# An adaLN block on one core: the second layer norm of tiles 4 to 7 moved from the first half into the second half's first pass

## The chip, the core and the metric

The kernel runs on one core of one Trainium2 chip. A core has TensorE (PE, matmuls into PSUM), VectorE (DVE), ScalarE (ACT), GpSimd (POOL) and SyncE (SP, which only issues DMAs here). Each engine takes its own instructions in order; they meet at semaphores. The metric is the device time of one execution in microseconds.

## The reference

```python
mod = (_silu(c) @ wmod).reshape(B, 6, 1, -1)             # sa, ca, ga, sb, cb, gb for each of 4 batches
h = _layernorm(x) * (1 + ca) + sa
q = h @ Wq.T;  sigma_q = elu(q) + 1                       # 16 heads of 32
a = einsum('bhsd,nhde->nbhse', sigma_q, memories) / clip(einsum('bhsd,nhd->nbhs', sigma_q, memory_norms), 1e-6)
attn = einsum('nbhse,hn->bhse', a, softmax(bank_weights)) @ Wo.T
x = x + ga * attn
h = _layernorm(x) * (1 + cb) + sb                         # the second norm
h = silu(h @ w_gate) * (h @ w_up)
h = h where it is one of the two largest of its group of 4, else 0
x = x + gb * (h @ w_down)
```

x is 4 x 1024 tokens of 512 floats, the hidden size of the FFN 2048. Everything is float32; the kernel splits each factor into a high and a low part and adds three products (high x high, low x high, high x low).

## The kernel before, in words

The 4096 tokens are 8 tiles of 512, a tile is four subtiles of 128. The program has two halves, and each engine's order is written out by hand.

**First half (attention, 0 to about 320 us).** `tile(t)` runs once per tile on every engine, some 35.2 us each. TensorE makes the products with the norms, then for each subtile the four memory banks (`banks_of`), the transpose of their sum (`comb_transpose`) and the product with Wo (`wo_product`), and q of the next tile. VectorE scales the banks (L1065, `banks_r`), splits off the low part of the transposed sum (L1030, `combT_lo`), and adds the result into x (L1019 and L1024). POOL sums the banks (L469, L474). The second norm of tile t-1 runs inside tile t: `late_stats` (L889, bn_stats of a subtile) and `ln_aggregate` (L893) on VectorE, `ln_sqrt` (L566), `normalize` (L560) and `split_bits` (L610, which puts the two 16-bit halves of each float into separate columns) on ScalarE. SP then stores the bits to DRAM, from where a transposing DMA brings them back in the second half. Tile 7's norm is finished beside the first matmuls of the second half.

**Second half (FFN, from about 304 us).** There are 16 passes `tile_b(t2)` of 65.3 us: tiles 0 to 7 with hidden columns 0 to 1023 (passes 0 to 7), then again with 1024 to 2047. A pass has two chunks (cc = 0, 1). For each, TensorE makes four pairs of gate and up products (`gate_or_up`, j = 0 to 3, two pairs of banks used in turn) and, one chunk behind, the down product (`down`). ScalarE takes silu of a gate (L789), VectorE multiplies with up (L1157), ScalarE takes the absolute value (L795), and when all four are there VectorE finds the two largest of each four (`sparsify`, L1179 to L1198). ScalarE (L774) and POOL (L506) split the result for `down`. The inputs of the next tile, h2, are joined from the transposed bits on ScalarE (`join_h2`, L747 and L751) during the pass. Their high part (`h2_high`, L757) can only be written when the pass's last up product has been read, and POOL makes the low part (`h2_low`, L457, `h_lo` in the trace) while TensorE is in the last down product. Pass 0 is written out apart; it also splits the weights of the first two chunks (`split_w`, L739, as `w_raw` arrives).

SP issues its DMAs in order, each behind its waits: a load that stands behind `store_bits(t)` waits until ScalarE has copied the bits of tile t.

## Time and profile before

| | us |
|---|---|
| median of 3 runs | 1367.31 |
| lowest and highest | 1366.39, 1367.68 |
| the profiled execution, its own time | 1366.45 |
| its span (first to last instruction) | 1364.6 |
| TensorE busy / VectorE / ScalarE / POOL | 1341.1 / 847.0 / 637.8 / 564.3 |

The span is what the trace covers; the execution's own time is 1.85 us more. Matmuls are pipelined, so each is drawn longer (0.39 us) than the step to the next (0.226 us): a gap in TensorE's stream is read from the starts, not from the busy time. The granted TensorE clock is 0.999 of full speed over the span.

### The profile page before, as it was taken

To read this page: it belongs to the slowest core of one execution; us is meant where nothing else is said; L and a number is where in the kernel's file an instruction comes from. 1 tells how busy PE (TensorE), PEld (TensorE's weight loads), DVE (VectorE), ACT (ScalarE), POOL (GpSimd) and SP (SyncE) were. 2 spreads that over 40 slices of the span, in tenths; PEclk is the share of its full clock that TensorE was granted. 3 is DMA by queue.
4 is the path that set the end of the run, shared out by engine and by line. 5 is a ranking of instruction groups with operands and counts; after the bars stand their busy time and mean duration, and the time that the engine had idled before them with its cause. 6 is when DMAs were issued, how large, how long until landed. Compare 5 with 4: busy or idle time off the path is not lost.

```text
span 1364.6 us, 18637 instructions
## 1 busy us (share of the span) xinstructions
PE 1341.1 (98%) x6726; PEld 1098.6 (81%) x6726; DVE 847.0 (62%) x1220; ACT 637.8 (47%) x933; POOL 564.3 (41%) x428
## 2 busy tenths in 40 slices
PE   7899999999999999999999999999999999999998
PEld 6777777777788888888888888888888888888887
DVE  6878888886746364645555575765555646363646
ACT  6677777787543343434343444433333333343321
POOL 2877777770733141414141456543232323231412
PEclk9999999999999999999999999999999999999999
DMA  6422222136202020202030322322020202020102
GB/s 256 155 93 93 92 92 81 73 93 222 79 16 85 15 85 15 85 15 85 27 88 31 100 89 89 110 68 85 15 85 15 85 15 85 15 85 15 69 0 100
DMA packets 91422, 102.43 MB, mean 75 GB/s; under 512 B 68960, under 2 KB 69504, under 8 KB 84864
## 3 DMA queue, kind: packets, MB, share of 16 engines
q1 hardware_dynamic: 91392, 102.05, 23.0%
q8 instruction: 16, 0.26, 0.1%
q14 instruction: 14, 0.11, 0.0%
HBM read 51.69 MB, written 33.57 MB: 62 GB/s over the span
## 4 chain that ended last, share of the span: by engine, by line
PE 86%; DVE 8%; ACT 2%; issue 2%; POOL 1%; DMA 1%; SPq 0%; DVEq 0%; ACTq 0%; POOLq 0%
PE bank L1252 27%; PE bank L1254 27%; PE bank L1253 27%; DVE banks_r L1065 3%; PE bank L1327 2%; PE bank L1339 1%; DVE inv_norm L1053 1%; POOL h_lo L457 1%; PE bank L1280 1%; DMA wmod_sb<-in_wmod_dram 1%; PE bank L1303 1%; DVE ln_raw L889 0%; DVE h_abs L1198 0%; DVE combT_lo L1030 0%; DVE xn L985 0%
## 5 line engine op out<-in xcount | busy, mean ns | idle before, releaser
L1157 DVE TENSOR_TENSOR h_act<-bank,silu_g 128x512 f32<-128x512 f32 x128 | 88.3, 690 | 411.8 <-PE bank L1254 385.7
L506 POOL TENSOR_TENSOR hs_lo<-h_abs,hs_hi 128x512 fp32r<-128x512 f32 x124 | 170.0, 1401 | 381.4 <-ACT hs_hi L774 381.4
L774 ACT ACTIVATE hs_hi<-h_abs 128x512 fp32r<-128x512 f32 x124 | 72.7, 627 | 323.7 <-DVE h_abs L1198 200.8
L457 POOL TENSOR_TENSOR h_lo<-h_raw,h_hi 128x512 fp32r<-128x512 f32 x62 | 122.2, 1999 | 233.2 <-ACT h_hi L757 233.2
L1252 PE MATMUL bank<-h_hi,gate_w_hi 128*128 128x512 f32 x512 | 199.7, 390 | 1.8 <-POOL h_lo L457 1.5
L1252 PE MATMUL bank<-h_hi,up_w_hi 128*128 128x512 f32 x512 | 199.5, 390 | 0.7 <-DVE h_act L1157 0.7
L1253 PE MATMUL bank<-h_lo,gate_w_hi 128*128 128x512 f32 x512 | 199.2, 389 | 0.0
L1253 PE MATMUL bank<-h_lo,up_w_hi 128*128 128x512 f32 x512 | 199.2, 389 | 0.0
L1254 PE MATMUL bank<-h_hi,up_w_lo 128*128 128x512 f32 x512 | 199.2, 389 | 0.0
L1254 PE MATMUL bank<-h_hi,gate_w_lo 128*128 128x512 f32 x512 | 199.2, 389 | 0.0
L1252 PE MATMUL bank<-down_w_hi,hs_hi 128*128 128x512 f32 x496 | 192.9, 389 | 0.0
L1253 PE MATMUL bank<-down_w_lo,hs_hi 128*128 128x512 f32 x496 | 192.9, 389 | 0.0
L1254 PE MATMUL bank<-down_w_hi,hs_lo 128*128 128x512 f32 x496 | 192.9, 389 | 0.0
L789 ACT ACTIVATE silu_g<-bank 128x512 f32<-128x512 f32 x128 | 75.9, 595 | 216.7 <-PE bank L1254 216.6
L1252 PEld LDWEIGHTS bank<-h_hi,gate_w_hi 128*128 128x128 f32 x512 | 96.2, 188 | 23.5 <-POOL h_lo L457 2.3
L1252 PEld LDWEIGHTS bank<-h_hi,up_w_hi 128*128 128x128 f32 x512 | 96.1, 188 | 21.6 <-DVE h_act L1157 1.1
L1254 PEld LDWEIGHTS bank<-h_hi,up_w_lo 128*128 128x128 f32 x512 | 96.2, 188 | 20.0
L1254 PEld LDWEIGHTS bank<-h_hi,gate_w_lo 128*128 128x128 f32 x512 | 96.1, 188 | 20.0
L1253 PEld LDWEIGHTS bank<-h_lo,up_w_hi 128*128 128x128 f32 x512 | 96.1, 188 | 19.9
L1253 PEld LDWEIGHTS bank<-h_lo,gate_w_hi 128*128 128x128 f32 x512 | 96.1, 188 | 19.6
L795 ACT ACTIVATE h_abs<-h_act 128x512 f32<-128x512 f32 x128 | 80.0, 625 | 68.0 <-DVE h_act L1157 68.0
L1254 PEld LDWEIGHTS bank<-down_w_hi,hs_lo 128*128 128x128 f32 x496 | 93.1, 188 | 19.3
(149 smaller groups left out, 2472.7 us busy)
## 6 DMA issues: line engine op xcount, KB each, us to landing
x_ring<-in_x_dram SPq DMA_DIRECT2D x8, 1024.0 KB, 4.9
x_scratch<-x_ring SPq DMA_DIRECT2D x8, 1024.0 KB, 3.9
xn_bits_scratch<-set_up_stage SPq DMA_DIRECT2D x8, 1024.0 KB, 4.5
over_x<-x_scratch SPq DMA_DIRECT2D x8, 1024.0 KB, 4.9
acc_scratch<-over_x SPq DMA_DIRECT2D x8, 1024.0 KB, 3.9
over_x<-acc_scratch SPq DMA_DIRECT2D x8, 1024.0 KB, 4.9
out_dram<-over_x SPq DMA_DIRECT2D x7, 1024.0 KB, 3.9
w_raw<-in_w_gate_dram SPq DMA_DIRECT2D x4, 1024.0 KB, 6.0
```

The lines of the kernel that those rows point to most:

```text
L457: nc.gpsimd.tensor_tensor(h2_lo[:, k], h2_raw[:, k], h2_hi[:, k].bitcast(F32), ALU.subtract).then_inc(h2_lo_done, 1)
L506: nc.gpsimd.tensor_tensor(hs_lo[:, j], h_abs[:, j], hs_hi[:, j].bitcast(F32), ALU.subtract).then_inc(hs_lo_done, 1)
L774: nc.scalar.activation(hs_hi[:, j], h_abs[:, j], ACT.Copy).then_inc(hs_hi_done, 1)
L789: nc.scalar.activation(silu_g[:, j % 2], bank[2 * (j % 2)][:], ACT.Silu).then_inc(silu_done, 1)
L795: nc.scalar.activation(h_abs[:, j], h_act[:, cc, j], ACT.Abs).then_inc(abs_done, 1)
L1053: nc.vector.reciprocal(inv, inv).then_inc(recip_done, 1)
L1065: nc.vector.tensor_tensor(scaled[:, g // 2, :, g % 2], bank[g][:].rearrange("p (i a e) -> p i a e", i=2, e=DH), r[:, g // 2, :, g % 2].uns ...
L1157: nc.vector.tensor_tensor(h_act[:, cc, j], bank[2 * (j % 2) + 1][:], silu_g[:, j % 2], ALU.mult).then_inc(h_done, 1)
L1252: nc.tensor.matmul(out_, stat[0], mov[0], start=start, stop=False)
L1253: nc.tensor.matmul(out_, stat[0], mov[1], start=False, stop=False)
L1254: return nc.tensor.matmul(out_, stat[1], mov[0], start=False, stop=stop)
L1327: ins = nc.tensor.matmul(bank[2 * two + pair][:, cols], stat[rows, g, toks], mov[rows, g], start=first, stop=last)
```

## The change

`EARLY = 4` divides the tiles. Tiles 0 to 3 keep their second norm in the first half (in tiles 1 to 4 of the loop, `norm2`). Tiles 4 to 7 get none there: no statistics, root, normalization or bit copies, and SP's loads and stores no longer wait for them. Instead pass t2 of the second half (t2 = 1 to 4) prepares tile t2 + 3, one subtile after the other in one buffer `late_x1`, in these steps: ScalarE issues a load of 256 KB of x1 from DRAM (`late_load`); VectorE takes statistics (`late_norm`); ScalarE takes the root (`late_root`); VectorE the reciprocal and shift (`late_scalars`); ScalarE normalizes, copies the bits, and issues their store and the next load (`late_split`). The loops of ScalarE and VectorE are divided in two for it, and `load_bits` waits for the four stores of a tile. `eps_col` moves to memory that lives through both halves.

```diff
@@ -173,6 +174,14 @@
         up_w[1] = in_halves("up_w1", [P, K, J, P])
         down_w[0] = in_halves("down_w0", [P, J, D])
         down_w[1] = in_halves("down_w1", [P, J, D])
+        late_x1 = sbb("late_x1", [P, D])
+        late_raw = sbb("late_raw", [P, 6])
+        late_mv = sbb("late_mv", [P, 2])
+        late_sd = sbb("late_sd", [P, 1])
+        late_rstd = sbb("late_rstd", [P, 1])
+        late_shift = sbb("late_shift", [P, 1])
+        late_pad = sbb("late_pad", [P, 1])
+        late_bits = over_x1_rest[:, 3].bitcast(U16)
 
 
         small_in, norm_in, wq_in, wo_in = map(sem, ("small_in", "norm_in", "wq_in", "wo_in"))
...
@@ -299,8 +308,10 @@
                 sp.wait_ge(bits_done, 4 * t + 4)
                 sp.dma_start(bits_dram[t].rearrange("(s p) c -> p s c", p=P), xn2_bits).then_inc(bits_out, 16)
 
-            def load_bits(t2, half, tile=None):
+            def load_bits(t2, half, tile=None, late=False):
                 tile = t2 if tile is None else tile
+                if late:
+                    sp.wait_ge(bits_out, 64 * tile + 16 * (4 - 3 * EARLY))
                 sp.dma_start(bitsT.rearrange("p k h n -> p (k h) n"), bits_dram[tile][:, half * D:(half + 1) * D],
                              transpose=True).then_inc(bits_in, 16)
 
...
@@ -316,24 +327,24 @@
                                  transpose=True).then_inc(bits_in, 16)
                 store_x1(t - 1)
                 if t + 2 < NT:
-                    sp.wait_ge(xn2_done, 4 * t)
+                    if t <= EARLY:
+                        sp.wait_ge(xn2_done, 4 * t)
                     sp.wait_ge(x1_out, 16 * t)
                     sp.dma_start(x_ring[:, place(t + 2)], x_t[t + 2]).then_inc(x_in[place(t + 2)], 16)
                 if t == 1:
                     sp.wait_ge(w_lo_dve, 1)
                     load_w((0, 1))
                 if t == NT - 1:
-                    sp.wait_ge(xn2_done, 4 * t)
                     sp.wait_ge(x1_out, 16 * t)
                     load_w((1, 1))
                     sp.wait_ge(w_lo_dve, 2)
                     load_w((1, 0))
-                store_bits(t - 1)
+                if t <= EARLY:
+                    store_bits(t - 1)
             store_x1(NT - 1)
-            sp.wait_ge(xn2_done, 4 * NT)
             sp.wait_ge(x1_out, 16 * NT)
+            sp.wait_ge(bits_out, 16 * EARLY)
             load_bits(1, 0)
-            store_bits(NT - 1)
 
 
             sp.wait_ge(w_lo_dve, 3)
...
@@ -362,7 +373,7 @@
                 store_y(acc_t, t - 1, t - 1)
                 load_y(x1_t, t)
                 sp.wait_ge(bits_joined, 4 * t + 8)
-                load_bits(t + 2, 0)
+                load_bits(t + 2, 0, late=True)
 
             t = NT - 2
             sp.wait_ge(bits_joined, 4 * t + 6)
...
@@ -699,16 +710,13 @@
                             transposed()
                         else:
                             h1_split(t + 1, before_last=transposed, part=None if first else 1)
-                        if not first and not last:
+                        if norm2:
                             ln_sqrt(t - 1, 1)
                             normalize(t - 1, 1, xn2, xn2_done)
                     if s == 3:
-                        if not first and not last:
+                        if norm2:
                             split_bits(t - 1, (0, 1))
                         transposed()
-                        if last:
-                            normalize(t - 1, 1, xn2, xn2_done)
-                            split_bits(t - 1, (0, 1))
 
                     if last and s == 0:
                         for k in (0, 1):
...
@@ -760,7 +764,9 @@
 
             act.wait_ge(wa_lo, 1)
             act.wait_ge(mods_ready, 2)
-            with act.Fori(1, NT - 1) as t:
+            with act.Fori(1, EARLY + 1) as t:
+                tile(t, norm2=True)
+            with act.Fori(EARLY + 1, NT - 1) as t:
                 tile(t)
             tile(NT - 1, last=True)
             combT_high(4 * NT - 1, 1)
...
@@ -805,36 +811,76 @@
                     if j in between:
                         between[j]()
 
-            def tile_b(t2, tile=None, last=False):
+            def late_load(tile, s):
+                act.wait_ge(bits_done, 4 * tile + s)
+                nc.scalar.dma_start(late_x1[:], x1_t[tile, :, s]).then_inc(late_in, 16)
+
+            def late_root(tile, s):
+                act.wait_ge(ag2_done, 4 * tile + s + 1)
+                nc.scalar.activation(late_sd[:], late_mv[:, 1:2], ACT.Sqrt, bias=eps_col[:]).then_inc(sd_done[1], 1)
+
+            def late_split(tile, s):
+                index = 4 * tile + s - 3 * EARLY
+                act.wait_ge(shift_done[1], index + 1)
+                nc.scalar.activation(late_x1[:], late_x1[:], ACT.Identity, bias=late_shift[:],
+                                     scale=late_rstd[:]).then_inc(xn2_done, 1)
+                act.wait_ge(xn2_done, 4 * tile + s + 1)
+                act.wait_ge(bits_out, 16 * index)
+                words = late_x1[:].bitcast(U16).rearrange("p (k d h) -> p k h d", k=K, h=2)
+                nc.scalar.activation(late_bits.rearrange("p (k h d) -> p k h d", k=K, h=2), words,
+                                     ACT.Copy).then_inc(bits_done, 1)
+                act.wait_ge(bits_done, 4 * tile + s + 1)
+                nc.scalar.dma_start(bits_dram[tile][s * P:(s + 1) * P], late_bits).then_inc(bits_out, 16)
+                if s < S - 1:
+                    late_load(tile, s + 1)
+
+            def tile_b(t2, tile=None, last=False, late=False):
                 def join(k):
                     return lambda: join_h2(t2 + 1, tile, k)
 
+                def between(cc):
+                    if last:
+                        return {}
+                    if not late:
+                        return {0: join(2 * cc), 1: join(2 * cc + 1)}
+
+                    def join_and_root():
+                        join_h2(t2 + 1, tile, 2 * cc)
+                        late_root(t2 + 3, 2 * cc)
+
+                    def join_and_split():
+                        join_h2(t2 + 1, tile, 2 * cc + 1)
+                        late_split(t2 + 3, 2 * cc)
+
+                    return {0: join_and_root, 1: join_and_split, 3: lambda: late_root(t2 + 3, 2 * cc + 1)}
+
+                if late:
+                    late_load(t2 + 3, 0)
                 hs_high(2 * t2 - 1)
-                item(2 * t2, 0, {} if last else {0: join(0), 1: join(1)})
+                item(2 * t2, 0, between(0))
+                if late:
+                    late_split(t2 + 3, 1)
                 hs_high(2 * t2)
-                item(2 * t2 + 1, 1, {} if last else {0: join(2), 1: join(3)})
+                item(2 * t2 + 1, 1, between(1))
                 if not last:
                     act.wait_ge(up_done, 8 * t2 + 8)
                     h2_high(t2 + 1)
-
-            last_tile = NT - 1
+                if late:
+                    late_split(t2 + 3, 3)
+
             silu(0, 0, first=True)
-            ln_sqrt(last_tile, 1)
             silu(0, 1, first=True)
-            normalize(last_tile, 1, xn2, xn2_done)
             split_w(SPLITS[2])
             absolute(0, 0, 0, first=True)
-            split_bits(last_tile, (0, 1))
             silu(0, 2)
             absolute(0, 0, 1, first=True)
-            split_bits(last_tile, (2, 3))
             act.wait_ge(x1_done, 4 * NT)
             split_w(SPLITS[3])
             silu(0, 3)
             absolute(0, 0, 2, first=True)
             absolute(0, 0, 3, first=True)
             silu(1, 0)
-            act.wait_ge(bits_out, 16 * NT)
+            act.wait_ge(bits_out, 16 * EARLY)
             split_w(SPLITS[4])
             silu(1, 1)
             join_h2(1, 1, 0)
...
@@ -1118,7 +1169,7 @@
                     combT_low(u, 0)
                     attn_rest(t - 1, 3, u - 1, stats=False)
                 scale_banks(u + 2, 0, first)
-                if not first:
+                if norm2:
                     late_stats(t - 1, 3, u - 1)
                     dve.wait_ge(bn2_done, 4 * t)
                     ln_aggregate(t - 1, 1, ag2_done)
...
@@ -1126,19 +1177,19 @@
                 if first:
                     dve.wait_ge(ga_in, 16 * B)
                 attn_rest(t, 0, u, stats=False)
-                if not first and not last:
+                if norm2:
                     ln_scalars(t - 1, 1)
 
                 scale_banks(u + 3, 1, first)
                 if last:
-                    ln_scalars(t - 1, 1)
                     dve.wait_ge(h2_lo_done, 2)
                     for k in (2, 3):
                         dve.wait_ge(h2_hi_done, k + 1)
                         nc.vector.tensor_tensor(h2_lo[:, k], h2_raw[:, k], h2_hi[:, k].bitcast(F32),
                                                 ALU.subtract).then_inc(h2_lo_done, 1)
-                late_stats(t, 0, u)
-                attn_rest(t, 1, u + 1, between=lambda: combT_low(u + 2, 0))
+                if t < EARLY:
+                    late_stats(t, 0, u)
+                attn_rest(t, 1, u + 1, between=lambda: combT_low(u + 2, 0), stats=t < EARLY)
                 if first:
                     dve.wait_ge(mods_mm, 2)
                     nc.vector.tensor_copy(mods[:, 2], mm2[:, 0])
...
@@ -1208,28 +1259,48 @@
                     dve.wait_ge(y_scaled, 4 * t2 + s + 1)
                     nc.vector.tensor_tensor(y[:, s], bank[4 + s][:], y[:, s], ALU.add).then_inc(y_done, 1)
 
-            def tile_b(t2, last=False):
+            def late_norm(tile, s):
+                dve.wait_ge(late_in, 16 * (4 * (tile - EARLY) + s + 1))
+                nc.vector.bn_stats(late_raw[:], late_x1[:]).then_inc(bn2_done, 1)
+                dve.wait_ge(bn2_done, 4 * tile + s + 1)
+                nc.vector.memset(late_pad[:], 0.0)
+                nc.vector.bn_aggr(late_mv[:], late_raw[:]).then_inc(ag2_done, 1)
+
+            def late_scalars(tile, s):
+                index = 4 * tile + s - 3 * EARLY
+                dve.wait_ge(sd_done[1], index + 1)
+                nc.vector.reciprocal(late_rstd[:], late_sd[:]).then_inc(rstd_done[1], 1)
+                dve.wait_ge(rstd_done[1], index + 1)
+                nc.vector.scalar_tensor_tensor(out=late_shift[:], in0=late_mv[:, 0:1], scalar=-1.0, in1=late_rstd[:],
+                                               op0=ALU.mult, op1=ALU.mult).then_inc(shift_done[1], 1)
+
+            def tile_b(t2, last=False, late=False):
                 for cc in range(SLOTS):
                     n = 2 * t2 + cc
                     for j in range(J):
                         hidden_act(n, cc, j)
+                        if late and j == 0:
+                            late_norm(t2 + 3, 2 * cc)
                         if cc == 1 and j == 1:
                             add_ffn(t2 - 1)
+                        if late and j == 1:
+                            late_scalars(t2 + 3, 2 * cc)
+                        if late and j == 3:
+                            late_norm(t2 + 3, 2 * cc + 1)
                     if last and cc == 1:
                         for half in range(2):
                             sparsify(n, cc, toks=LAST_HALVES[half], half=half)
+                    elif late:
+                        sparsify(n, cc, between=lambda: late_scalars(t2 + 3, 2 * cc + 1))
                     else:
                         sparsify(n, cc)
 
 
             split_w_low(SPLITS[1])
-            attn_rest(NT - 1, 2, 4 * NT - 2)
+            attn_rest(NT - 1, 2, 4 * NT - 2, stats=False)
             combT_low(4 * NT - 1, 1)
             hidden_act(0, 0, 0)
-            attn_rest(NT - 1, 3, 4 * NT - 1)
-            dve.wait_ge(bn2_done, 4 * NT)
-            ln_aggregate(NT - 1, 1, ag2_done)
-            ln_scalars(NT - 1, 1)
+            attn_rest(NT - 1, 3, 4 * NT - 1, stats=False)
             hidden_act(0, 0, 1)
             split_w_low(SPLITS[2])
             hidden_act(0, 0, 2)
...
@@ -1239,7 +1310,9 @@
             for j in range(1, J):
                 hidden_act(1, 1, j)
             sparsify(1, 1)
-            with dve.Fori(1, NT2 - 1) as t2:
+            with dve.Fori(EARLY - 3, NT - 3) as t2:
+                tile_b(t2, late=True)
+            with dve.Fori(NT - 3, NT2 - 1) as t2:
                 tile_b(t2)
             tile_b(NT2 - 1, last=True)
             add_ffn(NT2 - 1)
```

**VectorE, last tile of the first half,** from the scaling of the last banks to the low part of the first up weights (`up_w_lo`). Before:

```order
L1065 TENSOR_TENSOR banks_r<-bank,inv_norm 128x2x256 x4
L898 RECIPROCAL ln_rstd<-ln_sd 128x4
L900 SCALAR_TENSOR_TENSOR ln_shift<-ln_mv,ln_rstd 128x4
L1138 TENSOR_TENSOR h_lo<-h_raw,h_hi 128x512 x2
L889 BN_STATS ln_raw<-x_ring 128x6
L1019 TENSOR_TENSOR bank<-bank,ga_all 128x512
L1030 TENSOR_TENSOR combT_lo<-bank,combT_hi 128x512
L1024 TENSOR_TENSOR x_ring<-bank,x_ring 128x512
L889 BN_STATS ln_raw<-x_ring 128x6
L1037 TENSOR_TENSOR up_w_lo<-w_raw,up_w_hi 128x2048
```

Now (line numbers of the changed kernel):

```order
L1114 TENSOR_TENSOR banks_r<-bank,inv_norm 128x2x256 x4
L1188 TENSOR_TENSOR h_lo<-h_raw,h_hi 128x512 x2
L1068 TENSOR_TENSOR bank<-bank,ga_all 128x512
L1079 TENSOR_TENSOR combT_lo<-bank,combT_hi 128x512
L1073 TENSOR_TENSOR x_ring<-bank,x_ring 128x512
L1086 TENSOR_TENSOR up_w_lo<-w_raw,up_w_hi 128x2048
```

The scalars of tile 6 and two statistics of tile 7 are gone; what is left keeps its order.

**ScalarE, end of a pass of the second half,** from the last absolute values to the jump back (h_hi is h2's high part for the next tile). Before:

```order
L795 ACTIVATE h_abs<-h_act 128x512 x2
L817 ISA
L757 ACTIVATE h_hi<-h_raw 128x512 x4
L847 REGISTER_ALU
L847 COMPARE_AND_BRANCH
```

Now, in passes 1 to 4:

```order
L801 ACTIVATE h_abs<-h_act 128x512 x2
L819 REGISTER_ALU
L820 ACT_TABLE_LOAD
L820 ACTIVATE late_sd<-late_mv,eps_col 128x1
L866 ISA
L761 ACTIVATE h_hi<-h_raw 128x512 x4
L824 REGISTER_ALU
L825 ACTIVATE late_x<-late_x,late_shift,late_rstd 128x512
L828 REGISTER_ALU
L830 ACTIVATE over_x<-late_x 128x1024
L833 ISA
L833 DMA xn_bits_scratch<-over_x 128x1024
```

A table load and a root stand in front of h_hi, and a normalization, a bit copy and a store behind it.

**ScalarE, start of the next pass,** from the loop's entry to the first silu. Before:

```order
L774 ACTIVATE hs_hi<-h_abs 128x512
L786 ISA
L788 REGISTER_ALU
L789 ACTIVATE silu_g<-bank 128x512
```

Now:

```order
L816 DMA late_x<-x_scratch 128x512
L777 ISA
L779 REGISTER_ALU
L780 ACT_TABLE_LOAD
L780 ACTIVATE hs_hi<-h_abs 128x512
...
L792 ISA
L794 REGISTER_ALU
L795 ACT_TABLE_LOAD
L795 ACTIVATE silu_g<-bank 128x512
```

The load of the first subtile and two table loads are new here (the first also in passes 5 and 6). One of four hs_hi is shown.

## Rows read from the trace of the kernel before

**Rows 1.** The page, busy times (1) and the chain that ended last (4), by engine.

```profile
PE 1341.1 (98%) x6726; PEld 1098.6 (81%) x6726; DVE 847.0 (62%) x1220; ACT 637.8 (47%) x933; POOL 564.3 (41%) x428
...
PE 86%; DVE 8%; ACT 2%; issue 2%; POOL 1%; DMA 1%; SPq 0%; DVEq 0%; ACTq 0%; POOLq 0%
```

**Rows 2.** Stretches: start:end us, length, busy us (instructions), TensorE clock, DMA share, GB/s.

```profile
400.00:500.00 100.00, 100.00 (x443) 82.84 (x442) 55.17 (x67) 37.08 (x56) 31.86 (x20) 1.00 0.20 63
...
420.00:424.00 4.00, 4.00 (x19) 3.30 (x19) 0.00 (x0) 1.12 (x2) 0.00 (x0) 1.00 0.63 262
```

**Rows 3.** TensorE in order of time: start, us, engine, line, operation [idle <- releaser].

```profile
224.47 0.28 PE L1327 MATMUL bank<-mem_lo,sigma_hi 64*128 64x256 f32 x2
224.85 0.50 PE L1252 MATMUL bank<-wo_hi,combT_hi 128*128 128x512 f32 x1
...
336.40 0.50 PE L1252 MATMUL bank<-h_hi,up_w_hi 128*128 128x512 f32 x1
```

**Rows 4.** The same view, the four large gaps.

```profile
308.17 0.51 PE L1252 MATMUL bank<-wo_hi,combT_hi 128*128 128x512 f32 x1 [0.82 <-DVE combT_lo L1030]
...
353.70 0.50 PE L1252 MATMUL bank<-h_hi,up_w_hi 128*128 128x512 f32 x1 [0.68 <-DVE h_act L1157]
...
368.56 0.39 PE L1254 MATMUL bank<-h_hi,gate_w_lo 128*128 128x512 f32 x1
369.69 0.50 PE L1252 MATMUL bank<-h_hi,gate_w_hi 128*128 128x512 f32 x1 [0.74 <-POOL h_lo L457]
...
371.38 0.50 PE L1252 MATMUL bank<-h_hi,gate_w_hi 128*128 128x512 f32 x1 [0.72 <-POOL h_lo L457]
```

**Rows 5.** VectorE, ScalarE and POOL in order of time, where those gaps come from.

```profile
306.25 0.68 DVE L889 BATCH_NORM_STATS2 ln_raw<-x_ring 128x6 f32<-128x512 f32 x1
...
340.66 1.92 ACT L739 ACTIVATE down_w_hi<-w_raw 128x2048 fp32r<-128x2048 f32 x1 [2.56 <-DMA w_raw<-in_w_down_dram]
...
363.38 7.94 POOL L457 TENSOR_TENSOR h_lo<-h_raw,h_hi 128x512 fp32r<-128x512 f32 x4 [1.69 <-ACT h_hi L757]
```

**Rows 6.** Groups by shape: count | busy us, mean ns | idle before.

```profile
L610 ACT ACTIVATE set_up_stage<-xn 128x1024 uint16<-128x1024 uint16 x32 | 31.7, 1042 | 0.0
...
L566 ACT ACT_TABLE_LOAD x10 | 12.8, 1283 | 0.2
...
L560 ACT ACTIVATE xn<-x_ring,ln_shift,ln_rstd 128x512 f32<-128x512 f32 x16 | 11.7, 803 | 4.6 <-DVE ln_shift L900 4.6
...
L893 DVE BATCH_NORM_AGGREGATE ln_mv<-ln_raw 128x2 f32<-128x6 f32 x64 | 6.0, 156 | 0.3
...
L566 ACT ACTIVATE ln_sd<-ln_mv,eps_col 128x4 f32<-128x4 f32 x16 | 4.7, 292 | 10.1 <-DVE ln_mv L893 10.0
```

**Rows 7.** SP's queue at 419.51 (issue time), and DMA issues: KB each, us to landing.

```profile
419.51 0.37 SPq L349 DMA_DIRECT2D acc_scratch<-over_x  x1
...
over_x<-gates_scratch SPq DMA_DIRECT2D x16, 256.0 KB, 5.8
...
out_dram<-over_x SPq DMA_DIRECT2D x4, 256.0 KB, 2.5
```

**Rows 8.** The end of pass 1 and start of pass 2, in order of time, three engines.

```profile
425.44 2.18 ACT L757 ACTIVATE h_hi<-h_raw 128x512 fp32r<-128x512 f32 x4
...
426.13 7.98 POOL L457 TENSOR_TENSOR h_lo<-h_raw,h_hi 128x512 fp32r<-128x512 f32 x4 [18.04 <-ACT h_hi L757]
...
436.83 0.39 PE L1252 MATMUL bank<-h_hi,gate_w_hi 128*128 128x512 f32 x1
...
441.45 0.58 ACT L789 ACTIVATE silu_g<-bank 128x512 f32<-128x512 f32 x1
...
445.67 0.39 PE L1252 MATMUL bank<-h_hi,gate_w_hi 128*128 128x512 f32 x1
```

**Rows 9.** ScalarE in order of time, around one table load.

```profile
203.16 1.28 ACT L620 ACT_TABLE_LOAD   x1
204.46 0.63 ACT L620 ACTIVATE exp_q<-exp_q 128x512 f32<-128x512 f32 x1
```

More of the change, by code:

```diff
@@ L48 @@
 SA, CA, GA, SB, CB, GB = range(6)
+EARLY = 4
 def adaln_kernel(nc, x, wqT, woT, bank_w, mem_hd, norm_hd, w_gate, w_up, w_down, cT, wmod, out):
@@ L78, in adaln_kernel @@
         mods = ctx.enter_context(nc.sbuf_tensor("mods", [P, 4, K, B], F32))
+        eps_col = ctx.enter_context(nc.sbuf_tensor("eps_col", [P, 1], F32))
         gate_w, up_w, down_w = [None] * SLOTS, [None] * SLOTS, [None] * SLOTS
@@ L137, in adaln_kernel @@
             ln_mv = sba("ln_mv", [P, 2, S, 2])
-            eps_col = sba("eps_col", [P, 1])
             ln_sd = sba("ln_sd", [P, 2, S])
@@ L203, in adaln_kernel @@
         wo_done, attn_scaled_done, x1_done = map(sem, ("wo_done", "attn_scaled_done", "x1_done"))
-        xn2_done, bits_done = map(sem, ("xn2_done", "bits_done"))
+        xn2_done, bits_done, late_in = map(sem, ("xn2_done", "bits_done", "late_in"))
         w_in = [sem(f"w_in{i}") for i in range(3 * CHUNKS)]
@@ L675, in copy_row, with tile @@
                 nc.scalar.activation(mod_rows[:, i], bank[5 + 2 * i][:, 0:P], ACT.Copy).then_inc(rows_done, 1)
-            def tile(t, first=False, last=False):
+            def tile(t, first=False, last=False, norm2=False):
                 for s in range(S):
@@ L721, in tile @@
                         h2_high(0, (s + 1,))
-                    if last and s == 2:
-                        ln_sqrt(t - 1, 1)
                     if first and s == 3:
@@ L727, in h2_rest @@
                 def h2_rest():
-                    if not first:
+                    if norm2:
                         split_bits(t - 1, (2, 3))
-                if last:
-                    h2_rest()
-                else:
+                if not last:
                     sigma_all(t + 1, between=h2_rest, before_high=lambda: combT_high(4 * t + 3, 1))
@@ L846, in _ @@
             h2_high(1)
-            with act.Fori(1, NT - 1) as t2:
+            act.wait_ge(x1_out, 16 * NT)
+            with act.Fori(EARLY - 3, NT - 3) as t2:
+                tile_b(t2, t2 + 1, late=True)
+            with act.Fori(NT - 3, NT - 1) as t2:
                 tile_b(t2, t2 + 1)
@@ L1074, in tile @@
                 u = 4 * t
+                norm2 = 1 <= t <= EARLY
                 def stats(*subtiles):
@@ L1107, in tile @@
                     scale_banks(u, 0, between=next_scalars)
-                    late_stats(t - 1, 2, u - 2)
+                    if norm2:
+                        late_stats(t - 1, 2, u - 2)
                 invert_norms(t, 1)
@@ L1120, in tile @@
                 scale_banks(u + 2, 0, first)
-                if not first:
+                if norm2:
                     late_stats(t - 1, 3, u - 1)
@@ L1128, in tile @@
                 attn_rest(t, 0, u, stats=False)
-                if not first and not last:
+                if norm2:
                     ln_scalars(t - 1, 1)
```

## The prediction

> **What bounds the kernel now.** I read the page's busy times and chain first, then the stretches, then TensorE's instructions in order of time, then the engines it waits for. TensorE is busy for 98% of the span and makes up 86% of the chain that ended last [rows 1]. From 400 us on it has no idle time, with a matmul every 0.226 us: 100.00 of 100 us for 443 of them [rows 2]; the waits that are listed for it lie before 372 us and in the last tile. So only two things can move the time: gaps in TensorE's stream before about 372 us, which the change may close, and new gaps in the second half, which it may open. The other engines have room: DVE 847 us, ScalarE (ACT) 638 us, GpSimd (POOL) 564 us of 1364.6 [rows 1].
>
> The gaps are read as steps between the starts of neighbouring matmuls, since the modelled ends hide short ones. Seven small ones lie where VectorE has a step of the second norm, or a weight split behind one, ahead of what TensorE waits for. The first of them is the step from 224.47 to 224.85, 0.38 us where 0.23 is usual, and the last is at 336.40 [rows 3]. With about 0.15 us each at 224.85, 260.05 and 294.96, 0.05 at 300.26, 0.3 at 306.38 and 311.69, and 0.2 at 336.40 they hold 1.3 us. The large ones are at 308.17 (0.82 us idle for combT_lo), 353.70 (0.68 for h_act), and 369.69 and 371.38 (0.74 and 0.72 for h_lo) [rows 4]. The last one's neighbour shows the true cost: from 368.56 to 369.69 is 1.13 us, 0.90 more than a usual step, and the first step behind a gap is another 0.1 longer. So these four cost 1.0, 0.95, 1.0 and 1.0 us.
>
> **What is removed.** In the first half tiles 4 to 7 lose 16 bn_stats of 0.68 us, 16 aggregates of 0.16, 16 normalizing activations of 0.80, 16 bit copies of 1.04 and four roots of 0.29 [rows 5, 6]. That is 13 us of VectorE and 31 us of ScalarE. Nearly all of it lies beside matmuls; only what stands in front of something late counts, and there are four places.
>
> 1. Tiles 5, 6 and 7: one bn_stats (0.68 us) stood between two groups of banks_r. Without it combT_lo comes in time, but the wait for POOL's combined stays, since POOL starts it from an earlier banks_r. I take the small gaps at 0.15, 0.15, 0.15 and 0.05 us.
> 2. Around 305 us VectorE runs scalars, h_lo, a bn_stats at 306.25, a product, and only then combT_lo [rows 5]. Without the statistics and the aggregate at 299 us, combT_lo ends near 306.8, not just before 308.17. TensorE is free near 306.8 too, so all of the 1.0 us at 308.17 goes, with 0.3 at 306.38 and 0.3 at 311.69, where up_w_lo was the last.
> 3. ScalarE spends 3.2 us from 322 us on normalizing tile 7 and 4.2 on its bit copies [rows 6], and SP issues its loads in order behind them: the first down weights are used at 340.66, after a wait of 2.56 us for their transfer [rows 5]. With both gone these weights are asked for near 324, so their split starts near 335 and ends near 337. The sparsification then starts 4 us earlier. VectorE still shares its time with POOL's weight split, ends near 348, and h_act is there before TensorE wants it at 351.0. The 0.95 us at 353.70 goes, and the 0.2 at 336.40.
> 4. The same chain brings POOL's four h_lo for tile 1 from 363.38 to about 359.0, while TensorE comes 2.7 us earlier. They take 7.94 us [rows 5], so the fourth ends at 367.0 and is wanted at 366.6. Of 2.0 us 0.4 stays and 1.6 goes.
>
> Sum of the gains: 1.3 + 1.0 + 0.95 + 1.6 = 4.85 us. From below this is 0 (something else is as late), from above 6 us: all 5.25 us of these gaps, and a little of those that POOL sets.
>
> **What is added.** Each of the four passes 1 to 4 of the second half now prepares a tile in four subtiles. ScalarE gets, per subtile, a root (0.29), a normalization (0.80), a bit copy (1.04), two DMA issues, and table loads of 1.28 us [rows 6, 7]. The order shows nine loads a pass: four for roots, four for silu behind them, one at the loop's start. One issue takes SP 0.37 us [rows 7]; ScalarE's own is not in the trace of before, and I take the same, with 0 below and 1.5 above. Per pass that is 9 x 1.28 + 4 x 2.13 + 8 x 0.37 = 23 us, on an engine that works some 24 of a pass's 65.3 us. VectorE gets 1.2 us per subtile. So neither becomes the bound; only the order matters. TensorE writes four banks in turn and needs a silu or product about 8 us after it has finished the matmuls for it, which covers 5 us of insertions in the middle of a pass. The tight place is the end of the pass, in two respects.
>
> **h_lo of the next tile.** Before, ScalarE goes from the last h_abs to h_hi at 425.44, POOL's four h_lo run from 426.13 to 434.11, and TensorE wants the fourth at 436.83 [rows 8]: 2.7 us of room. Now a table load and a root stand in front, 1.28 + 0.29 + 0.1 = 1.7 us, and h_lo ends near 435.9. Room left is 0.9 us. The root also waits for VectorE's statistics, which wait for the fourth subtile's transfer. ScalarE issues it near 422.6, behind the store of the third. The nearest rows are 2.5 us for 256 KB alone and 5.8 us for 256 KB issued behind 1 MB [rows 7]. I take 3.0, nearer to the first, since y's 1 MB load is issued only at 424: it lands near 425.6, the aggregate is there at 426.6, and the table load hides it.
>
> **The first silu of the next pass.** It starts at 441.45 now and is wanted at 445.67 [rows 8], where the third gate group starts: with its 0.6 us, 3.6 us of room. In front of it come 1.1 us of VectorE (statistics ahead of sparsification), 0.4 of scalars inside sparsification, 0.3 because ScalarE's last bit copy, two issues and the loop's table load run until about 440.5, and 1.28 for silu's own table. That is 3.1 us, and 0.5 is left.
>
> Both margins are smaller than what I can be wrong by, so I count 0.2 us lost per pass, 0.8 in all, with 0 and 9 as ends. Other waits are covered: the bits of a tile are written one pass before SP asks for them, and passes 5 and 6 get two table loads each, with 3.6 us of room.
>
> **A rule weighed.** At 203.16 a table load takes 1.28 us and the exponential starts at 204.46, 0.02 us behind it [rows 9]. So here a switch costs 1.3 us. The Trainium skill (ScalarE: Activation LUTs, What ACT_TABLE_LOAD costs) puts a drain of 1380 ns on top of the load, 2.66 us for each switch. By that rule the added loads would cost 96 us instead of 46, and both margins would be gone; the trace disagrees with it.
>
> **Sum.** The profiled execution took 1366.45 us around a span of 1364.6. Less 4.85, plus 0.8, its own time becomes 1362.4. The median of the runs is 0.86 us above it, so I forecast 1363.3 us, 0.3% faster. Runs of this kernel differ by 1.3 us, so I call anything within 0.2% (2.7 us) no change.
>
> **Rivals.**
> - *The ends of the passes give it back* (0.22). If ScalarE's issues or the waits among the four handovers per subtile cost 1 us more than I took, TensorE waits about 1 us at each of four ends: 1363.3 + 4 = 1367. For it: margins of 0.5 to 0.9 us, and a chain in which each subtile waits for ScalarE, VectorE and a DMA in turn. Against it: VectorE and ScalarE catch up in the middle of a pass, so it doesn't add up.
> - *The fourth subtile lands late, and it is slower* (0.13). If its transfer shares the engines with y's store and load, as the gate row's did, it takes 5.8 us. It lands at 428.4, the root ends at 429.7, the fourth h_lo at 438.5: 1.6 us of waiting, and 0.6 more at the first silu. That is 2.2 us a pass, 8.8 in all, so 1367.3 - 4.85 + 8.8 = 1371. It decides from a landing of 4.2 us on. For it: the DMA engines are 63% busy from 420 to 424 us in the trace [rows 2]. Against it: the queued 1 MB is not in front but behind.
> - *A table switch holds ScalarE about twice as long as its load* (0.03). With 1.3 us more for each, h_lo is late by 0.4 and silu, behind three switches, by 3.4 beyond its room: 3.5 us a pass, 14 in all, 1376. The pair at 203.16 speaks against it. This is the time that the rule of the Trainium skill (ScalarE: Activation LUTs, What ACT_TABLE_LOAD costs) would make.
> - *The gaps before 372 us stay* (0.07). If loads from HBM and not ScalarE set the down weights' arrival, the 0.95 and 1.6 us stay, and 2.3 - 0.8 = 1.5 us are gained: 1365.8.
> - *My forecast*, 1361 to 1364.6, has 0.55.
>
> Its own range is 1361.0 to 1364.6. The range over the cases is 1360.6 to 1370.5. Chances: faster 0.59 (the forecast, and a part of the first and fourth rivals), same 0.25, slower 0.16.
>
> **What would show it.** In the new profile no idle time in front of combT_lo's product near 308, none near 352 and 370 or at most 0.5 us; ScalarE's down_w_hi near 335; nine table loads a pass of 1.28 us; POOL's fourth h_lo ending within 1 us of the gate group that reads it; PE waits in four places at a distance of 65 us, short or absent. I am wrong if TensorE waits over 1 us at each of these, if a DMA issue on ScalarE takes over 1 us, or if the gaps before 372 us are still there.

## The result and the profile after

The changed kernel takes 1374.97 us (median of 5 runs, 1371.39 to 1375.59) against 1367.09 us (1366.39 to 1367.68) before: a ratio of 1.0050, with a 95% interval of 1.0039 to 1.0062. It is slower, where 1363.3 us and 0.3% faster were forecast. It lies outside the forecast's own range of 1361.0 to 1364.6 and outside the range over the cases, 1360.6 to 1370.5. The profiled execution took 1371.39 us around a span of 1369.6, the fastest of the five. The other four have no trace: in them up to 4.2 us more were lost, and where is not shown.

The page's busy times of the changed kernel and its chain that ended last, against [rows 1]:

```profile
PE 1344.3 (98%) x6726; PEld 1099.2 (80%) x6726; DVE 850.3 (62%) x1260; ACT 693.1 (51%) x982; POOL 561.3 (41%) x428
...
PE 66%; issue 18%; POOL 7%; DVE 6%; ACT 2%; DMA 1%; POOLq 0%; ACTq 0%; SPq 0%; DVEq 0%
```

ScalarE (ACT) has 55 us more of work, and TensorE's share of the chain fell from 86 to 66%. The stretches of [rows 2] show where:

```profile
400.00:500.00 100.00, 97.99 (x430) 80.19 (x429) 60.15 (x95) 65.57 (x86) 29.13 (x19) 1.00 0.33 94
...
420.00:424.00 4.00, 4.00 (x20) 3.30 (x19) 0.69 (x1) 3.03 (x4) 0.00 (x0) 1.00 0.78 197
```

TensorE made 443 matmuls in these 100 us before and makes 430 now, at the same full clock: 13 x 0.226 = 2.9 us are missing. From 700 us on it is back at 443. So the loss lies in passes 1 to 4, those that prepare a late tile. TensorE in order of time, at the first place of [rows 4] and around the start of pass 2 ([rows 8]):

```profile
306.07 0.50 PE L1325 MATMUL bank<-h_hi,gate_w_hi 128*128 128x512 f32 x1 [0.18 <-DVE h_lo L1188]
...
307.27 0.50 PE L1325 MATMUL bank<-wo_hi,combT_hi 128*128 128x512 f32 x1 [0.24 <-DVE combT_lo L1079]
...
433.31 0.50 PE L1325 MATMUL bank<-h_hi,gate_w_hi 128*128 128x512 f32 x1 [0.55 <-POOL h_lo L468]
...
434.99 0.50 PE L1325 MATMUL bank<-h_hi,gate_w_hi 128*128 128x512 f32 x1 [0.71 <-POOL h_lo L468]
...
444.87 0.50 PE L1325 MATMUL bank<-h_hi,gate_w_hi 128*128 128x512 f32 x1 [0.75 <-ACT silu_g L795]
```

The gap at 353.70 is gone, of the two near 370 one step is left that is 0.30 us longer than usual (at 367.37), and that at 308 is down to 0.24. In their place pass 1 ends with two waits for h_lo, at 433.31 and 434.99, and passes 2, 3 and 4 with one each (0.72 at 502.40, 0.69 at 569.73, 0.70 at 637.17). The third gate group of the next pass waits for silu at 444.87, 512.28 and 579.60 (0.73 to 0.75 us each). By the starts each of these costs 0.70 to 0.91 us. From the list of TensorE's waits by releaser (us in total, times, longest) of the changed kernel:

```profile
...
PE bank L1325 <- POOL h_lo L468: 3.4, 5, 0.7
PE bank L1412 <- POOL combined L485: 3.1, 8, 1.1
PE bank L1325 <- ACT silu_g L795: 2.7, 5, 0.8
```

What holds them, at the end of pass 1, in order of time (ACTq and SPq rows are DMA issues; L355 is the load of y, L816 that of a subtile):

```profile
419.95 0.37 ACTq L816 DMA_DIRECT2D late_x<-x_scratch  x1
420.00 0.35 SPq L355 DMA_DIRECT2D over_x<-x_scratch  x1
420.49 0.60 ACT L795 ACTIVATE silu_g<-bank 128x512 f32<-128x512 f32 x1 [1.23 <-issue]
...
425.62 0.69 DVE L1264 BATCH_NORM_STATS2 late_raw<-late_x 128x6 f32<-128x512 f32 x1 [3.81 <-DMA late_x<-x_scratch]
...
426.46 1.19 DVE L1230 TENSOR_TENSOR pair_hi<-h_abs 128x1024 f32<-128x1024 f32 x1
426.57 0.29 ACT L820 ACTIVATE late_sd<-late_mv,eps_col 128x1 f32<-128x1 f32 x1 [2.79 <-DVE late_mv L1267]
426.78 2.18 ACT L761 ACTIVATE h_hi<-h_raw 128x512 fp32r<-128x512 f32 x4
427.47 7.46 POOL L468 TENSOR_TENSOR h_lo<-h_raw,h_hi 128x512 fp32r<-128x512 f32 x4 [19.01 <-ACT h_hi L761]
427.57 2.32 DVE L1231 TENSOR_TENSOR pair_lo<-h_abs 128x1024 f32<-128x1024 f32 x1
...
435.79 0.82 ACT L825 ACTIVATE late_x<-late_x,late_shift,late_rstd 128x512 f32<-128x512 f32 x1 [6.83 <-DVE late_shift L1274]
...
438.87 0.35 ACTq L816 DMA_DIRECT2D late_x<-x_scratch  x1
439.41 1.28 ACT L780 ACT_TABLE_LOAD   x1 [1.64 <-issue]
440.71 2.20 ACT L780 ACTIVATE hs_hi<-h_abs 128x512 fp32r<-128x512 f32 x4
...
442.92 1.28 ACT L795 ACT_TABLE_LOAD   x1
444.22 1.09 ACT L795 ACTIVATE silu_g<-bank 128x512 f32<-128x512 f32 x2
```

The load of the fourth subtile and y's load leave within 0.05 us of each other. In the next three passes they are 0.24, 0.23 and 0.20 us apart, and the landings are 5.05 to 5.11 us: a pass that is late moves both, and they meet again. VectorE stands idle for the subtile until 425.62, 5.67 us behind the issue. Two things queue behind it: on ScalarE the root and then h2_high, on VectorE the whole sparsification. From bn_stats to the next pass's first silu, 18.60 us, every step waits for the one before: sparsification beside GpSimd's h_lo, normalise, bit copy, two issues, a table load, hs_hi, a second table load.

### The profile page after: what moved, and what is told of

The parts are those of the page before. It is cut to its first block, busy times and chain, and to the rows that moved or that the text cites. A ratio compares the mean times of both kernels' runs of the same rounds, so it can differ in the third digit from the quotient of the medians.

```text
span 1369.6 us, 18878 instructions
## 1 busy us (share of the span) xinstructions
PE 1344.3 (98%) x6726; PEld 1099.2 (80%) x6726; DVE 850.3 (62%) x1260; ACT 693.1 (51%) x982; POOL 561.3 (41%) x428
## 4 chain that ended last, share of the span: by engine, by line
PE 66%; issue 18%; POOL 7%; DVE 6%; ACT 2%; DMA 1%; POOLq 0%; ACTq 0%; SPq 0%; DVEq 0%
PE bank L1325 21%; PE bank L1327 21%; PE bank L1326 20%; POOL hs_lo L517 2%; POOL h_lo L468 2%; DVE banks_r L1114 2%; PE bank L1400 2%; PE bank L1412 1%; POOL sigma_lo L453 1%; POOL banks_r L480 1%; PE bank L1353 1%; DMA wmod_sb<-in_wmod_dram 1%; DVE h_abs L1249 0%; POOL combined L485 0%; DVE inv_norm L1102 0%
## 5 line engine op out<-in xcount | busy, mean ns | idle before, releaser
L1326 PEld LDWEIGHTS bank<-down_w_lo,hs_hi 128*128 128x128 f32 x496 | 93.1, 188 | 19.4
```

The costliest lines, as they stand in the source:

```text
L1326: nc.tensor.matmul(out_, stat[0], mov[1], start=False, stop=False)
```

## The experiments

All are compared with the kernel before on the same chip; the changed kernel was not run again beside them. The kernel before had medians of 1366.97 us (first four), 1367.16 (next three) and 1367.17 (last). "Landing" below is the time from the fourth subtile's issue on ScalarE to its bn_stats in pass 1, "chain" from there to the next first silu, "period" the step between passes in the trace. A "..." in an edit marks lines left out.

**first_half_only**: the late loops take the ordinary passes.

```diff
...
+                sp.dma_start(bits_dram[t + EARLY].rearrange("(s p) c -> p s c", p=P), xn2_bits).then_inc(late_in, 16)
...
-            with act.Fori(EARLY - 3, NT - 3) as t2:
-                tile_b(t2, t2 + 1, late=True)
-            with act.Fori(NT - 3, NT - 1) as t2:
+            with act.Fori(EARLY - 3, NT - 1) as t2:
...
```

> Leaves out the late steps of passes 1 to 4 (their loads, norms and bits stores); tiles 4 to 7 get no second norm of their own, the bits of tiles 0 to 3 are stored twice in their place, so that the second half has words to load. Theory: the first half gained what was forecast (4.85 us) and all of the loss is in passes 1 to 4, so without the late steps the time is 1362.3 us (1361.5 to 1363.5). Rival: the first half gained nothing that lasts to the end, and the time is that of before, 1367 us. Second rival: the first half itself is slower, over 1368 us.

Measured: 1362.79 us, ratio 0.9971 (0.9959 to 0.9984), period 65.28 us as before. The first half brought 4.2 us (1366.97 - 1362.79; 3.8 by the spans) and keeps it, where 4.85 were forecast. So the whole loss is made by the late steps: 8.8 us between the spans of this kernel (1360.8) and of the changed one (1369.6), 12 us between the medians. Only the profiled execution has a trace, so the 3.4 us between these two numbers stay without a cause.

**one_load**: the four subtiles come by one transfer at the start of the pass.

```diff
-        late_x1 = sbb("late_x1", [P, D])
+        late_x1 = w_raw[:].rearrange("p (s d) -> p s d", d=D)
...
-                nc.scalar.dma_start(late_x1[:], x1_t[tile, :, s]).then_inc(late_in, 16)
+                nc.scalar.dma_start(late_x1, x1_t[tile]).then_inc(late_in, 16)
...
-                if s < S - 1:
-                    late_load(tile, s + 1)
```

> The changed kernel with the whole x1 of a late tile fetched by one transfer at the start of the pass, into the weight staging that is free then: no subtile waits for its transfer, and three DMA issues per pass leave ScalarE. Theory (the late landing of the fourth subtile and the chain behind it cost the time): VectorE's waits of 3.8 and 3.3 us for late_x1 go, h2_high and sparsify start some 3 us earlier, both kinds of TensorE waits (h_lo, silu_g) go, and the time falls from 1375 to 1363 to 1366 us. Rival (ScalarE's added work itself, 16 normalises, copies, roots and table loads, costs it): only the three issues of about 0.5 us per pass go, 4 x 1.5 = 6 us of ScalarE at most and most of it in its idle time, so 1371 us or more.

Measured: 1363.35 us, ratio 0.9973 (0.9962 to 0.9983). VectorE in order of time in this kernel:

```profile
420.57 0.69 DVE L1207 TENSOR_TENSOR h_act<-bank,silu_g 128x512 f32<-128x512 f32 x1 [3.90 <-PE bank L1326]
421.18 0.68 DVE L1263 BATCH_NORM_STATS2 late_raw<-w_raw 128x6 f32<-128x512 f32 x1
```

No wait stands ahead of the fourth bn_stats, 4.4 us earlier than in the changed kernel. TensorE's waits for POOL's h_lo are off its list and those for silu_g down to 0.5 us in all, of which 0.2 at the start of pass 1. All sixteen roots, normalisations, bit copies and stores are still there, so ScalarE's work as such costs at most 0.6 us (1363.35 against the 1362.79 without late steps).

**high_first**: h2_high ahead of the fourth root.

```diff
+                    def high_and_root():
+                        if cc == 1:
+                            act.wait_ge(up_done, 8 * t2 + 8)
+                            h2_high(t2 + 1)
+                        late_root(t2 + 3, 2 * cc + 1)
...
-                if not last:
+                if not last and not late:
                     act.wait_ge(up_done, 8 * t2 + 8)
                     h2_high(t2 + 1)
```

> The changed kernel with h2_high ahead of the fourth subtile's root instead of behind it. Theory (late landing): the landing stays at 5 to 5.7 us, but TensorE's waits for h_lo (3.4 us over four passes in the trace) go; those for silu_g (2.7 us) stay or grow by up to 1 us a pass, since the root now comes 8.8 us later and holds VectorE's scalars in sparsify. Time 1370 to 1373 us. Rival (ScalarE's work as such): no change, 1374 to 1376 us.

Measured: 1363.58 us, ratio 0.9975 (0.9965 to 0.9984): better than the 1370 to 1373 expected, although the landing grew to 6.76 us (the load leaves 0.05 us behind y's here). VectorE and GpSimd (POOL) in this kernel:

```profile
423.33 5.04 POOL L468 TENSOR_TENSOR h_lo<-h_raw,h_hi 128x512 fp32r<-128x512 f32 x4 [14.59 <-ACT h_hi L761]
...
426.97 0.69 DVE L1270 BATCH_NORM_STATS2 late_raw<-late_x 128x6 f32<-128x512 f32 x1 [4.91 <-DMA late_x<-x_scratch]
...
429.37 1.21 DVE L1237 TENSOR_TENSOR pair_lo<-h_abs 128x1024 f32<-128x1024 f32 x1
...
431.64 0.68 DVE L1240 TENSOR_TENSOR both_of<-pair_lo,pair_hi 128x512 bf16<-128x512 f32 x1
```

I had expected silu to stay late. What I missed is that h_lo now falls into VectorE's wait for the transfer and is nearly over when sparsification starts. From pair_hi to the first both_of takes 3.84 us here (427.80 to 431.64) and 5.58 in the changed kernel (426.46 to 432.04), and the four h_lo take 5.04 against 7.46 us. The two both_of themselves take 0.68 us each instead of 1.76 and 1.75. Together VectorE is 3.9 us shorter from pair_hi to the scalars behind both_of (427.80 to 432.84, against 426.46 to 435.40), and that is what the chain lost: it fell from 18.60 to 14.68 us.

**y_after**: y's store waits for the fourth bn_stats, and with it y's load and what SP issues behind that.

```diff
             def store_y(dst, tile, t2, after=0):
+                if not isinstance(after, int):
+                    sp.wait_ge(bn2_done, after)
                 sp.wait_ge(y_done, 4 * t2 + 4)
...
-                store_y(acc_t, t - 1, t - 1)
+                store_y(acc_t, t - 1, t - 1, after=4 * t + 16)
```

> The changed kernel with the store and load of y in passes 1 to 4 held back until VectorE has read the fourth subtile. Theory (the 1 MB transfer of y shares the DMA engines with the 256 KB one): the fourth landing falls from 5.0 to 5.7 us to 3.1 to 3.6 us, h_lo's waits go and silu_g's shrink, time 1367 to 1371 us. Rival (the landing is late whatever else moves): landing still over 5 us, 1374 to 1376 us. Second rival: y's load now collides with the next steps (weights, bits of the next pass) and the time grows.

Measured: 1366.29 us, ratio 0.9996 (0.9987 to 1.0005), just below the 1367 to 1371 expected. Landing 3.52 us, and no wait for h_lo is left in the late passes. The chain is 18.62 us, and silu is still late, which the theory's estimate had allowed for; TensorE in this kernel:

```profile
443.03 0.50 PE L1335 MATMUL bank<-h_hi,gate_w_hi 128*128 128x512 f32 x1 [0.56 <-ACT silu_g L805]
```

The period is 66.1 us. So y's transfers, or those that SP issues behind them, make the landing late, and even with a landing of 3.5 us the first silu has no room.

**both**: the edits of one_load and high_first together.

> The single transfer of one_load and the order of high_first together. Theory: each alone already took TensorE's waits in the late passes down to 0.5 us, so nothing is left to gain: 1363 to 1364 us, as each alone. Rival (the two remove different losses that add): 1360 to 1361.5 us, below the kernel without late steps less its noise.

Measured: 1363.42 us, ratio 0.9973 (0.9963 to 0.9983), the same as each alone. The losses that they remove do not add.

**no_tables**: the root is left out, the table loads go with it.

```diff
-                nc.scalar.activation(late_sd[:], late_mv[:, 1:2], ACT.Sqrt, bias=eps_col[:]).then_inc(sd_done[1], 1)
+                nc.scalar.activation(late_sd[:], late_mv[:, 1:2], ACT.Identity, bias=eps_col[:]).then_inc(sd_done[1], 1)
```

> The changed kernel with the square root of the late norms left out: ScalarE copies the variance with eps added, so VectorE takes the reciprocal of that, and no table is loaded in the late passes. Theory (the fourth landing and GpSimd's h_lo beside sparsify cost the time): the load ahead of the fourth root lies in the wait for the landing, so h_lo's waits stay (3.4 us); the two loads of 1.28 us ahead of hs_high and the first silu leave that chain, its waits (2.7 us) go: 1371 to 1373 us. Rival (the sixteen roots with up to 1.28 us twice are the main cost): 1364 to 1367 us.

Measured: 1363.58 us, ratio 0.9975 (0.9966 to 0.9984). The theory's number was wrong; the rival's, 1364 to 1367, is nearer, and the time lies just below it. Landing is 5.07 us, but the issue comes 0.87 us earlier (419.08), and the chain is 15.94 us, 2.66 shorter, two table loads of 1.28. That is not proof that table loads are the main cost, since high_first and load_first keep all of them and come out at the same time: it is the same chain, shortened at another place.

**load_first**: the next subtile's load is issued ahead of the store.

```diff
                 act.wait_ge(bits_done, 4 * tile + s + 1)
+                if s < S - 1:
+                    nc.scalar.dma_start(late_x1[:], x1_t[tile, :, s + 1]).then_inc(late_in, 16)
                 nc.scalar.dma_start(bits_dram[tile][s * P:(s + 1) * P], late_bits).then_inc(bits_out, 16)
-                if s < S - 1:
-                    late_load(tile, s + 1)
```

> The changed kernel with each subtile's load issued ahead of the bits store of the one before, not behind it: the load leaves 0.5 us earlier. Theory: loss follows the fourth landing (1.9 us earlier brought 8.7 us over four passes in y_after), so 0.5 us earlier bring 1.5 to 2.5 us: 1372 to 1373.5 us. Rival (what counts is only whether the transfer of y is beside it, or the load now slows the store): 1375 us, no change.

Measured: 1363.70 us, ratio 0.9976 (0.9966 to 0.9985), far more than the 0.5 us of the edit. The issues in this kernel, and VectorE's wait:

```profile
419.51 0.34 ACTq L834 DMA_DIRECT2D late_x<-x_scratch  x1
...
420.87 0.35 SPq L355 DMA_DIRECT2D over_x<-x_scratch  x1
...
423.36 0.69 DVE L1264 BATCH_NORM_STATS2 late_raw<-late_x 128x6 f32<-128x512 f32 x1 [1.18 <-DMA late_x<-x_scratch]
```

The subtile's load now leaves 1.36 us ahead of y's, and lands in 3.85 us instead of 5.67; the chain is as long as ever (18.65 us). In the other three passes the leads are 1.33 to 1.37 us and the landings 3.69 to 3.95, and the late passes have none of TensorE's waits for h_lo.

The lead is larger than the 0.5 us of the edit, and why is seen when both kernels are counted from the same matmul, TensorE's gate product at 306.07 in the changed kernel and 306.92 here (in this execution TensorE was 0.85 us later even before the second half). From there the fourth subtile's load leaves after 112.59 us instead of 113.88, so 1.29 us earlier. Some 0.5 us of that is the new order. The rest comes from the second subtile of the pass, whose load leaves 0.56 us earlier by the same edit. VectorE's wait for it falls from 1.68 to 0.85 us:

```profile
392.89 0.70 DVE L1264 BATCH_NORM_STATS2 late_raw<-late_x 128x6 f32<-128x512 f32 x1 [0.85 <-DMA late_x<-x_scratch]
```

ScalarE keeps that to the copy of the third subtile, which ends 0.76 us earlier by this count. So the middle of a pass had hardly any slack either: what one subtile loses there, the next ones carry on. Expected were 1.5 to 2.5 us of gain; neither this nor how sharply the landing depends on who issues first was in either theory.

**y_load_after**: as y_after, but y's store leaves at its usual time, and y's load and what SP issues behind it wait.

```diff
                 sp.wait_ge(y_out, 16 * (t2 + 1))
+                if not isinstance(after, int):
+                    sp.wait_ge(bn2_done, after)
...
-                store_y(acc_t, t - 1, t - 1)
+                store_y(acc_t, t - 1, t - 1, after=2 * (2 * t + 8))
```

> As y_after, but only the load of y is held back until VectorE has read the fourth subtile; the store of y leaves at its usual time, some 3.5 us ahead of the fourth subtile's load. It tells which of y's two transfers made the landing late. If it is the load: landing 3.5 to 3.9 us as in y_after, the first silu of a pass some 18.6 us behind the fourth bn_stats, time 1363.5 to 1366.5 us. If it is the tail of the store (3.9 us long, still under way when the load is issued): landing 4.5 us or more, time 1369 us or more.

Measured: 1365.84 us, ratio 0.9991 (0.9982 to 1.0001). Landing 3.56 us, chain 18.63: it is not the store. The first line of the edit shows why it could hardly have been: SP waits until the store has landed before it issues y's load, so at 420.00 in the changed kernel, 0.05 us behind the subtile's issue, the store was over. But SP issues in order, and two more transfers stand behind y's load, the 256 KB gate row and the transposing load of the bits. SP's queue in the changed kernel, then in this one:

```profile
420.00 0.35 SPq L355 DMA_DIRECT2D over_x<-x_scratch  x1
420.64 0.36 SPq L356 DMA_DIRECT2D over_x<-gates_scratch  x1
421.75 5.69 SPq L315 DMA_TRANSPOSE over_x<-xn_bits_scratch  x1
...
425.28 0.36 SPq L355 DMA_DIRECT2D over_x<-x_scratch  x1
425.91 0.35 SPq L356 DMA_DIRECT2D over_x<-gates_scratch  x1
427.01 4.64 SPq L315 DMA_TRANSPOSE over_x<-xn_bits_scratch  x1
```

Both experiments hold all three back, and load_first moves the subtile ahead of all three. So what is shown is that the group from y's load on makes the landing late; that y's 1 MB alone does it is likely by its size, but not shown.

Side by side, all for pass 1 but the median. "Silu" is the start of the next pass's first silu, counted from TensorE's gate product at 306 us in the same kernel:

| kernel | landing | chain | silu | period | median, us |
|---|---|---|---|---|---|
| changed | 5.67 | 18.60 | 138.15 | 67.4 | 1374.97 |
| y_after | 3.52 | 18.62 | 136.12 | 66.1 | 1366.29 |
| y_load_after | 3.56 | 18.63 | 136.13 | 66.0 | 1365.84 |
| load_first | 3.85 | 18.65 | 135.09 | 65.3 | 1363.70 |
| no_tables | 5.07 | 15.94 | 133.16 | 65.3 | 1363.58 |
| high_first | 6.76 | 14.68 | 135.39 | 65.4 | 1363.58 |
| both | no wait | 18.62 | 133.77 | 65.3 | 1363.42 |
| one_load | no wait | 18.41 | 133.59 | 65.3 | 1363.35 |

Up to a silu at 135.4 us the period stays at 65.3 to 65.4, and from 136.1 on it grows. Landing, chain and the moment of the issue add up to that one number, and each of the edits shortens another part of it.

Four kernels with all of the computation, one_load, both, high_first and load_first, are 0.24 to 0.27% faster than the kernel before. They stand within 1 us of the one without late steps, so at most 0.9 us more is to be had from these passes.

## Why the prediction was wrong, step by step

- *The gains of the first half*: right in mechanism, 4.2 us instead of 4.85. I had counted the gaps at 308.17 and 306.38 as all gone, but by the starts the steps that end at 307.27 and 306.07 are still 0.41 and 0.34 us longer than usual. ScalarE's down_w_hi came at 335.80 ("near 335"), and POOL's four h_lo for tile 1 start at 359.35 (forecast "around 359.0").

```profile
335.80 1.91 ACT L743 ACTIVATE down_w_hi<-w_raw 128x2048 fp32r<-128x2048 f32 x1
...
359.35 7.97 POOL L468 TENSOR_TENSOR h_lo<-h_raw,h_hi 128x512 fp32r<-128x512 f32 x4 [1.65 <-ACT h_hi L761]
```

- *The step that failed*: "I take 3.0, nearer to the first, since y's 1 MB load is issued only at 424". It was two errors. The issue came later: moved by the 4.0 us by which the changed kernel is ahead here, my 422.6 is 418.6, and it was 419.95. I had priced an issue at its row of 0.37 us, but the second of two starts 0.69 us behind the copy (419.26 to 419.95). That is 0.3 of the 1.35 us. At least 0.76 more came from the middle of the pass, which I had counted as covered: load_first won that much back by having the second subtile's load leave 0.56 us earlier. The rest is open, since the prediction has no sum for its 422.6. y's load came where I put it (424 - 4.0 = 420.0, measured 420.00). So the 1.4 us of lead that the argument needed was gone. And then a landing of 3.0 us became 5.67. load_first shows that with 1.36 us of lead it is 3.85, and even with y's load held back it is 3.46 to 3.93: the 3.0 was too short in any case.
- *h_lo*: with the root at 426.57 the fourth h_lo ended at 434.93, 3.0 us behind the forecast (435.9 - 4.0), and the room of 0.9 us was used up three times over.
- *The first silu*: forecast 0.5 us of room with an early landing; y_after, with an early landing, has TensorE wait 0.56. At the end of the pass I had priced two issues at 0.37 us each; the two there leave ScalarE idle for 1.64 us ahead of the loop's table load.
- *0.8 us lost in all* is the term that was mis-sized: 8.8 us in the profiled pair, 12 by the medians. My upper end of 9 us for it would have held the former, but with it the sum gives 1371.5 (1366.45 - 4.85 + 9 + 0.86), and two of the rivals stood at 1371 and 1376: the range over the cases, which ended at 1370.5, was too narrow by the prediction's own terms. The rival of the late landing had mechanism and size (2.2 us a pass, 8.8 in all, 1371) as the profiled execution has them (steps of 68.2, 67.4 and 67.3 us between the y loads of passes 1 to 4 instead of 65.3), and I gave it 0.13. What spoke against it, that the 1 MB is queued behind and not in front, was right (by 0.05 us) and did not help; it rested on a lead hardly longer than my error.
- *Table loads*: 16 for roots, 19 for silu, 6 for hs_hi, each 1283 ns, and where nothing else is waited for the next operation follows at once, as [rows 9] had it. Groups by shape of the changed kernel:

```profile
L795 ACT ACT_TABLE_LOAD x19 | 24.4, 1283 | 0.3
...
L820 ACT ACT_TABLE_LOAD x16 | 20.5, 1283 | 0.3
...
L1264 DVE BATCH_NORM_STATS2 late_raw<-late_x 128x6 f32<-128x512 f32 x16 | 11.0, 689 | 19.9 <-DMA late_x<-x_scratch 19.9
```

The longer switch, and with it that rival, was not there: 440.71 follows 439.41 by 1.30 us. Not tried was to take the last split of a pass out of the way of the next silu, or to hold back y's load alone with the two transfers behind it at their usual time.

## What to carry to other kernels

When several engines hand a small piece of work round and TensorE's feeders queue behind it, put what TensorE needs ahead of the step that waits, not behind it: the same transfer may then be late at no cost. Price a margin along the whole chain to the next operand, and if two transfers are issued within a microsecond or so of each other in the forecast, price the late landing too: here 0.2 us of lead gave 5.1 us and 1.36 us gave 3.85. If two small errors in one direction can use up the margin, the rival that does so deserves more than a small chance.

## What the runs showed of the hardware

- A 256 KB load that ScalarE issued within 0.05 us of a 1 MB load on SP's queue, itself followed by a 256 KB and a transposing load, was read 5.67 us later (6.08 to 6.83 over the four passes of high_first). With 0.20 to 0.24 us of lead it was 5.05 to 5.11, with 1.33 to 1.37 us 3.69 to 3.95, and with SP's three transfers held back 3.46 to 3.93. In no_tables, 1.26 to 1.30 us of lead by the start of the issue, but an issue of 0.90 us instead of 0.35, gave 4.98 to 5.21. Whether the lead counts from the issue's end is open, and so is why that issue was longer.
- VectorE's and GpSimd's two-operand work slow each other: pair_lo takes 2.32 us beside h_lo and 1.21 alone, four h_lo 6.97 to 7.98 beside sparsification and 5.04 when only their last 0.6 us meet it. The Trainium skill (SBUF — State Buffer, Who interferes with whom) says that a VectorE instruction with two SBUF inputs contends with a GpSimd instruction that reads SBUF; the traces agree, and they add that the price moves with the order: 1.7 us up to both_of, and 3.9 on the whole chain in high_first.
- Two DMA issues in a row, each with a row of 0.35 to 0.37 us, hold ScalarE for 1.23 us in the middle of a pass, and for 1.64 us at its end, where the next pass's first load is the second of them.
